# Loading a ring of weights in two transfers over 64 partitions each, instead of one over 128

## The chip, the cores and the metric

The kernel runs on one core of a Trainium2 chip. The metric is the device time of one execution, in microseconds. Before the change the median of three runs is 747.68 us (747.62 to 747.77).

## What is computed

The input is one image of 16 channels and 64 x 64 pixels in fp32. Four layers follow each other: a local normalisation with a blur of 13 x 13 (L0), a window attention block (L1), two 3 x 3 convolutions with a residual (L2), and the window attention block once more with other weights (L3). Almost all bytes of the problem are the weights of the two attention blocks. Cut to its matrix products, one block is:

```python
fl = _ln(xf, pn_g, pn_b)                          # 64 tokens of 1024
pw = _attn(fl, Wqk_p, PDH)                        # Wqk_p 1024 x 2048
pv = _heads(fl @ Wv_p)                            # Wv_p  1024 x 1024
pf = _merge(pw @ pv + _dwconv(pv, ...)) @ Wout_p  # Wout_p 1024 x 1024
ww = _attn(_ln(pl, pln_g, pln_b), Wqk_w, WDH)     # Wqk_w 1024 x 2048
wv = _heads(_ln(xw, wn_g, wn_b) @ Wv_w)           # 4 windows; Wv_w 16384 x 1024, 64 MB
wf = _merge(nds @ wv + _dwconv(wv, ...)) @ Wout_w # Wout_w 1024 x 16384, 64 MB
out = diag_scaled @ _heads(pf) + wf + x
```

## The kernel before

All weights are streamed from HBM once, in slots of 128 partitions x 2048 fp32 values (1 MB, 8 KB in each partition). One layer has 152 slots. `ring` in SBUF holds 16 of them, in two halves of 8 slots, b = 0 and b = 1; `extra` holds 4 more, for the first and the last slots ahead of the two big matrices. A load of a whole half is 128 rows of 64 KB, one for each partition, from one contiguous piece of 8.39 MB in HBM (`halves`). Some loads take half of a half (4 slots, 128 rows of 32 KB).

SP issues every DMA, all on one queue. Its program is written out by hand: `load_half` (line 268) waits for nothing itself; ahead of each call SP waits until PE has counted `slots_used` so far that the half is free. Each transfer counts up `half_landed[b]`, and a transfer that is whole adds 16. The other transfers of the program are: the first loads (`images`, `blurs`), five loads of `extra` from `ends`, the small inputs (`window_gains`, `small` over 104 partitions, `const`, `const_low` over 32, `l2w` over 16), six last pieces of the last matrix (`last`, over 128 partitions, line 305), two stores of `out` (28 partitions each) and two of `windows_last`. With the 37 ring loads that makes 59 transfers, 54 of them over 128 partitions.

PE works slot by slot. `half_there` (line 324) makes it wait on `half_landed[b]` before the first slot of a half. In the stage of Wv_w (line 490) each of 64 slots is multiplied by the staged window pixels and accumulated in one PSUM bank; in the stage of Wout_w (line 517) eight slots make a group, which ScalarE copies out (line 658), PE transposes (line 322) and VectorE adds to the image (line 937). After each slot PE counts up `slots_used`. The small first part of each layer (lines 386 to 474) works on the slots of the four small matrices, and between the two layers stands the convolution (lines 539 to 544).

Of the kernel before, what the change touches and what calls it, by code (L numbers as in the profile page):

```python
# [22 lines left out]
P = 128  # L23
# [10 lines left out]
SLOT = 2048  # L34
QUARTER = 4
HALF = 8
# [18 lines left out]
N_HALVES = (TURN + N_VW + N_OUTW) // HALF  # L55
# [5 lines left out]
def piece_at(n):  # L61

    at = sum(4 * (c1 - c0) * (h1 - h0) for c0, c1, h0, h1 in LAST_PIECES[:n])
    c0, c1, h0, h1 = LAST_PIECES[n]
    return at, at + 4 * (c1 - c0) * (h1 - h0)
# [52 lines left out]
def build(nc, images, blurs, const, const_low, window_gains, small, l2w, ends, halves, last, out, windows_last):  # L118
    with ExitStack() as ctx, ExitStack() as engines:
        def sb(name, *shape):  # L120
            return ctx.enter_context(nc.sbuf_tensor(name, list(shape), F32))

        def sem(name):
            return ctx.enter_context(nc.semaphore(name))


        ring = sb("ring", P, TURN * SLOT)
# [53 lines left out]
        half_landed = [sem(f"half_landed{b}") for b in range(2)]  # L181
# [50 lines left out]
        def used(L, s):  # L232

            return L * PER_LAYER + s
# [20 lines left out]
        @block.sync  # L255
        def _(sp):
            def load_end(L, n):
                lo = 0 if L or n else SLOT
                sp.dma_start(extra[:, lo:], ends[2 * L + n][:, lo:]).then_inc(extra_landed, 16)

            def load_small():
                sp.dma_start(area[0][:, :], window_gains).then_inc(gains_landed, 16)
                sp.dma_start(area[1][0:2 * N_SMALL, 0:P], small).then_inc(small_landed, 16)
                sp.dma_start(cst[:, C_WIDE:C_LOW], const).then_inc(const_landed, 16)
                sp.dma_start(cst[0:LOW, C_LOW:], const_low).then_inc(const_landed, 16)
                sp.dma_start(l2[:, :], l2w).then_inc(l2_landed, 16)

            def load_half(L, t, b, lo=0, hi=HALF):

                sp.dma_start(ring[:, (b * HALF + lo) * SLOT:(b * HALF + hi) * SLOT],  # L270
                             halves[t * 2 + (L * N_HALVES + 2 + b)][:, lo * SLOT:hi * SLOT]).then_inc(half_landed[b], 16)

            for L in range(2):
                load_end(L, 0)
                if L == 0:
                    load_small()
                if L:
                    sp.wait_ge(slots_used, used(L, -HALF))
                load_half(L, -1, 0)
                if L:  # L280
                    sp.wait_ge(slots_used, used(L, 0))
                else:
                    sp.wait_ge(image_turned, 1)
                load_half(L, -1, 1)
                sp.wait_ge(slots_used, used(L, QUARTER))
                load_end(L, 1)

                sp.wait_ge(slots_used, used(L, 2 * QUARTER))
                load_half(L, 0, 0, 0, QUARTER)
                sp.wait_ge(slots_used, used(L, 3 * QUARTER))  # L290
                load_half(L, 0, 0, QUARTER, HALF)
                sp.wait_ge(slots_used, used(L, 5 * QUARTER))
                load_half(L, 0, 1)
                with sp.Fori(1, 2 * TURNS - L) as t:
                    for b in range(2):
                        sp.wait_ge(slots_used, t * TURN + (used(L, S_VW) + b * HALF - HALF))
                        load_half(L, t, b)

            t = 2 * TURNS - 1
            sp.wait_ge(slots_used, used(1, S_VW) + t * TURN - HALF)  # L300
            load_half(1, t, 0)
            for n, landed in enumerate(last_landed):
                lo, hi = piece_at(n)
                sp.wait_ge(slots_used, used(1, S_VW) + t * TURN - HALF + (hi + SLOT - 1) // SLOT)
                sp.dma_start(ring[:, HALF * SLOT + lo:HALF * SLOT + hi], last[:, lo:hi]).then_inc(landed, 16)

            sp.wait_ge(rows_copied, 2)
            for wy in range(2):
                sp.dma_start(out[wy], out_rows[wy * WIN:wy * WIN + LAST, :]).then_inc(rows_stored, 16)
            sp.wait_ge(wide_copied, 1)  # L310
            sp.dma_start(windows_last[:, 0:WIDE], area[5][:, 0:WIDE]).then_inc(rows_stored, 16)
            sp.wait_ge(last_copied, 1)
            sp.dma_start(windows_last[:, WIDE:BANK], area[5][:, WIDE:BANK]).then_inc(last_stored, 16)
# [3 lines left out]
        def _(pe):  # L317
# [6 lines left out]
            def half_there(L, t, b):  # L324

                fills = (N_HALVES // 2 + 1, N_HALVES // 2)[b]
                before = 1 if t is None else (3, 2)[b]
                pe.wait_ge(half_landed[b], (0 if t is None else t) * 16 + 16 * (L * fills + before))

            def first_there(L, s):  # L330
                if s in (0, S_VW - QUARTER):
                    pe.wait_ge(extra_landed, 16 * (2 * L + (3 if s else 2)))
                elif s in (QUARTER, QUARTER + HALF):
                    half_there(L, None, s // HALF)
# [48 lines left out]
            with pe.Fori(0, 2) as L:  # L383
# [74 lines left out]
                for h in range(HEADS):  # L458
                    b, h2, hh, a = h % 2, h // 2, h // 4, h % 4 // 2
# [22 lines left out]
                with pe.Fori(0, TURNS) as i:  # L482
                    for k in range(TURN):
                        if k % HALF == 0:
                            pe.wait_ge(staged, i * 2 + (2 * TURNS * L + k // 8 + 1))
                            half_there(L, i, k // HALF)
                        w = slot_of(S_VW + k).rearrange("p (j n) -> p j n", j=4)
                        for j in range(4):
                            at = k % 8 * 8 + j // 2 * 4
                            m = mm(bank[0][32 * j:32 * j + 4, :], stage[:, k // 8, at:at + 4], w[:, j], start=False, stop=False)  # L490
                        m.then_inc(slots_used, 1)
# [17 lines left out]
                def group(L, i, g):  # L509
                    for h in range(GROUP):  # L510
                        if h == 0 and g == 0:
                            pe.wait_ge(wf_ready, L + 1)
                        if h == 0:
                            half_there(L, i + TURNS, g)
                        w = slot_of(S_OUTW + g * GROUP + h).rearrange("p (j n) -> p j n", j=4)
                        for j in range(4):
                            m = mm(bank[6 + g][32 * j:32 * j + 32, :], wf_t[:, h, :], w[:, j],  # L517
                                   start=(h == 0), stop=(h == GROUP - 1))
                        m.then_inc(slots_used, 1)
                    return m  # L520
# [494 lines left out]
```

## Time and profile before

| | |
|---|---|
| median of the runs | 747.68 us |
| the profiled execution, its own time | 747.75 us |
| its span in the profile | 746.4 us |
| mean granted TensorE clock | 0.783 |
| busy: PE, PE weight loads, VectorE, ScalarE, GpSimd | 58%, 17%, 12%, 5%, 1% of the span |
| DMA queue of the loads | 99.5% of 16 engines |
| moved | 320.51 MB, mean 429 GB/s |

The page of the profile divides the span in 40 slices of 18.7 us and gives each engine's busy share in tenths. A wait is put down to the work that ended it. The chain of work that ended last is followed back from the last instruction, at each step to what released it. Matmuls of fp32 data stand twice in the counts.

### The profile page before, as it was taken

The numbers are of one execution on the slowest core, as the hardware profiler recorded it, in microseconds if no ns is written. First come the engines' busy times: TensorE is split into PE (matmuls) and PEld (weight loads), VectorE is DVE, ScalarE is ACT, GpSimd is POOL, SyncE is SP. The second block draws the span as 40 slices with busy tenths as digits, with TensorE's granted clock in tenths as the row PEclk, the third lists the DMA queues.
The fourth block names the chain that finished last, engine by engine and source line by source line (L and its number), as shares of the span: only waits on it lengthen the run. The fifth ranks groups of instructions, "written<-read, shape, count | busy, mean of one in ns | idle before, by whom it ended". The sixth has DMA issues, their size and how long they took to land.

```text
span 746.4 us, 6899 instructions
## 1 busy us (share of the span) xinstructions
PE 430.1 (58%) x3011; PEld 129.0 (17%) x3011; DVE 90.9 (12%) x254; ACT 38.3 (5%) x80; POOL 9.3 (1%) x21
## 2 busy tenths in 40 slices
PE   6599854444446445455476988445444454544548
PEld 5233200000001111111122332000000011111113
DVE  2765300000002000000005171000000020000000
ACT  2111100000000000000001111000000000000000
POOL 2100000000000000000001000000000000000000
PEclk9579877777777776776789999877777777877879
DMA  9999999999999999999999999999999999999998
GB/s 396 436 403 429 459 411 439 443 439 421 435 446 412 435 440 443 425 428 446 418 432 443 417 431 446 446 421 425 446 435 421 439 446 421 425 446 435 421 423 350
DMA packets 8068, 320.51 MB, mean 429 GB/s; under 512 B 1065, under 2 KB 1601, under 8 KB 2169
## 3 DMA queue, kind: packets, MB, share of 16 engines
q1 hardware_dynamic: 8057, 320.35, 99.5%
q8 instruction: 8, 0.13, 0.1%
q14 instruction: 3, 0.02, 0.0%
HBM read 319.86 MB, written 0.49 MB: 429 GB/s over the span
## 4 chain that ended last, share of the span: by engine, by line
DMA 64%; PE 31%; DVE 3%; ACT 1%; issue 1%; SPq 0%; DVEq 0%; ACTq 0%
DMA ring<-halves 59%; PE bank L490 10%; PE bank L517 9%; PE bank L409 4%; DMA ring<-last 4%; PE bank L426 2%; PE bank L418 2%; DMA cst<-blurs 1%; PE bank L541 1%; PE bank L394 1%; PE bank L340 1%; PE bank L322 0%; DVE ring L724 0%; PE bank L386 0%; PE bank L539 0%
## 5 line engine op out<-in xcount | busy, mean ns | idle before, releaser
L490 PE MATMUL bank<-ring,stage 128*4 128x512 f32 x1024 | 140.8, 712 | 141.2 <-DMA ring<-halves 141.2
L517 PE MATMUL bank<-ring,wf_t 128*32 128x512 f32 x960 | 135.1, 726 | 128.4 <-DMA ring<-halves 128.4
L517 PEld LDWEIGHTS bank<-ring,wf_t 128*32 128x32 f32 x960 | 33.2, 131 | 219.9 <-DMA ring<-halves 121.8
L490 PEld LDWEIGHTS bank<-ring,stage 128*4 128x4 f32 x1024 | 26.9, 97 | 254.6 <-DMA ring<-halves 154.2
L937 DVE TENSOR_TENSOR image<-bank,image 128x32 f32 (+1 forms) x30 | 5.1, 193 | 275.9 <-PE bank L322 275.9
L902 DVE COPY wv_t<-bank 128x32 f32<-128x32 f32 x2 | 0.4, 190 | 286.6 <-PE bank L322 286.6
L322 PE MATMUL bank<-ident,area 128*128 128x128 f32 (+1 forms) x117 | 18.4, 284 | 12.2 <-ACT area L658 11.1
L658 ACT COPY area<-bank 128x512 f32<-128x512 f32 x15 | 8.8, 585 | 279.6 <-PE bank L517 279.6
L409 PE MATMUL bank<-extra,area 128*64 128x512 f32 x64 | 18.8, 752 | 3.8 <-DVE area L811 3.8
L474 PE MATMUL bank<-extra,area 128*64 128x512 f32 x64 | 18.4, 740 | 2.0 <-DVE area L876 2.0
L322 PEld LDWEIGHTS bank<-ident,area 128*128 128x128 f32 (+1 forms) x117 | 12.5, 141 | 31.7 <-ACT area L658 23.8
L646 ACT COPY stage<-area 128x64 f32 x16 | 3.9, 242 | 217.9 <-PE bank L490 203.8
L426 PE MATMUL bank<-ring,pooled_n 128*32 128x512 f32 x128 | 14.6, 595 | 0.0
L852 DVE SCALAR_TENSOR_TENSOR conv_p<-v_pad,vec,conv_p 128x636 f32<-128x636 f32 x16 | 14.1, 880 | 0.4
L418 PE MATMUL bank<-ring,area 128*64 128x512 f32 x64 | 14.1, 592 | 0.0
L409 PE MATMUL bank<-ring,area 128*64 128x512 f32 x64 | 14.1, 592 | 0.0
L561 PE MATMUL bank<-ring,wf_t 128*32 128x384 f32 (+1 forms) x128 | 7.9, 382 | 1.1 <-DMA ring<-last 1.1
L409 PEld LDWEIGHTS bank<-extra,area 128*64 128x64 f32 x64 | 5.6, 170 | 15.5 <-issue 15.5
L340 PE MATMUL bank<-cst,ring 128*128 128x128 f32 x16 | 3.8, 431 | 7.4 <-DMA cst<-blurs 7.4
L474 PEld LDWEIGHTS bank<-extra,area 128*64 128x64 f32 x64 | 5.5, 167 | 13.4 <-issue 13.4
L692 POOL TENSOR_TENSOR area<-area,vec 128x512 f32<-128x512 f32 x2 | 2.1, 1042 | 393.9 <-DVE area L786 393.9
L394 PE MATMUL bank<-area,ones 128*128 128x512 f32 x4 | 3.9, 1090 | 4.3 <-ACT area L612 4.3
(202 smaller groups left out, 206.8 us busy)
## 6 DMA issues: line engine op xcount, KB each, us to landing
ring<-halves SPq DMA_DIRECT2D x4, 4096.0 KB, 20.1
extra<-ends SPq DMA_DIRECT2D x3, 4096.0 KB, 16.4
extra<-ends SPq DMA_DIRECT2D x1, 3072.0 KB, 12.4
ring<-last SPq DMA_DIRECT2D x1, 3072.0 KB, 22.5
ring<-last SPq DMA_DIRECT2D x2, 1536.0 KB, 25.9
extra<-ends SPq DMA_DIRECT2D x1, 1024.0 KB, 4.9
ring<-last SPq DMA_DIRECT2D x1, 1024.0 KB, 28.9
ring<-last SPq DMA_DIRECT2D x1, 768.0 KB, 29.9
```

The lines of the kernel that those rows point to most:

```text
L322: return mm(dst, src, ident[0:rows, 0:rows], start=True, stop=True, is_transpose=True)
L340: m = mm(bank[pair // 4][:, pair % 4 * P:pair % 4 * P + P], l0_in[:, 2 * pair:2 * pair + 2, :].rearrange("p c x -> p (c x)"), cc("blur_y") ...
L394: mm(bank[0][:, :], ones, area[1][:, :], start=True, stop=True).then_inc(var_sums, 1)
L409: m = mm(bank[4 + m2][b * 64:b * 64 + 64, :], fl[:, s - S_QKP, :], w[:, m2, b], start=(s == S_QKP), stop=(s == S_VP - 1))
L418: m = mm(bank[6][b * 64:b * 64 + 64, :], fl[:, kt, :], w[:, t, b], start=(kt == 0), stop=(kt == KT - 1))
L426: m = mm(bank[7][32 * j:32 * j + 32, :], pooled_n[:, s - S_QKW, :], w[:, j * BANK:(j + 1) * BANK], start=(s == S_QKW), stop=(s == S_OUTP - 1))
L474: m = mm(bank[4][f * 64:f * 64 + 64, :], a3(8, TOK)[:, h, :], w[:, t, f], start=(h == 0), stop=(h == HEADS - 1))
L490: m = mm(bank[0][32 * j:32 * j + 4, :], stage[:, k // 8, at:at + 4], w[:, j], start=False, stop=False)
L517: m = mm(bank[6 + g][32 * j:32 * j + 32, :], wf_t[:, h, :], w[:, j], start=(h == 0), stop=(h == GROUP - 1))
L561: m = mm(dst, wf_t[:, h, :], w[:, h - h0, j], start=(h == 0 and c0 == 0), stop=(h == HEADS - 1))
L658: sc.copy(area[4 + g][:, :], bank[6 + g][:, :]).then_inc(group_copied, 1)
L852: then(v.scalar_tensor_tensor(conv_p[:, 0:159, 0:4], src, wt, conv_p[:, 0:159, 0:4], ALU.mult, ALU.add))
```

## The change

Each load of the ring is issued as two DMAs, one over partitions 0 to 63 and one over partitions 64 to 127, with the same columns, one right behind the other on SP's queue. Both count up the same semaphore, so PE now waits for 32 for each load instead of 16. Nothing else is changed; the loads of `extra`, the last pieces, the small inputs and the stores stay whole.

```diff
             def load_half(L, t, b, lo=0, hi=HALF):
 
-                sp.dma_start(ring[:, (b * HALF + lo) * SLOT:(b * HALF + hi) * SLOT],
-                             halves[t * 2 + (L * N_HALVES + 2 + b)][:, lo * SLOT:hi * SLOT]).then_inc(half_landed[b], 16)
+                for rows in (slice(0, P // 2), slice(P // 2, P)):
+                    sp.dma_start(ring[rows, (b * HALF + lo) * SLOT:(b * HALF + hi) * SLOT],
+                                 halves[t * 2 + (L * N_HALVES + 2 + b)][rows, lo * SLOT:hi * SLOT]).then_inc(half_landed[b], 16)
...
                 before = 1 if t is None else (3, 2)[b]
-                pe.wait_ge(half_landed[b], (0 if t is None else t) * 16 + 16 * (L * fills + before))
+                pe.wait_ge(half_landed[b], (0 if t is None else t) * 32 + 32 * (L * fills + before))
```

Before the change, the body of SP's loop over the ring (two halves; ISA and REGISTER_ALU are register instructions) and the load behind it read:

```order
L270 ISA [waits slots_used]
L270 DMA ring<-halves 128x16384
L296 REGISTER_ALU
L270 ISA [waits slots_used]
L270 DMA ring<-halves 128x16384
L294 REGISTER_ALU
L294 COMPARE_AND_BRANCH
L259 DMA extra<-ends 128x8192
```

With the change the same place on SP reads (every line number is one higher):

```order
L271 ISA [waits slots_used]
L271 DMA ring<-halves 64x16384
L271 ISA
L271 DMA ring<-halves 64x16384
L297 REGISTER_ALU
L271 ISA [waits slots_used]
L271 DMA ring<-halves 64x16384
L271 ISA
L271 DMA ring<-halves 64x16384
L295 REGISTER_ALU
L295 COMPARE_AND_BRANCH
L259 DMA extra<-ends 128x8192
```

Each wait on `slots_used` is followed by two transfers, with a register instruction between them. On the other engines no instruction moves.

## Rows read from the trace of the kernel before

**Rows 1.** The page: PE's busy time, and the DMA's share and rate by slice.

```profile
PE 430.1 (58%) x3011; PEld 129.0 (17%) x3011; DVE 90.9 (12%) x254; ACT 38.3 (5%) x80; POOL 9.3 (1%) x21
...
DMA  9999999999999999999999999999999999999998
GB/s 396 436 403 429 459 411 439 443 439 421 435 446 412 435 440 443 425 428 446 418 432 443 417 431 446 446 421 425 446 435 421 439 446 421 425 446 435 421 423 350
```

**Rows 2.** The page: DMA packets, and the queue of the loads.

```profile
DMA packets 8068, 320.51 MB, mean 429 GB/s; under 512 B 1065, under 2 KB 1601, under 8 KB 2169
...
q1 hardware_dynamic: 8057, 320.35, 99.5%
```

**Rows 3.** The page: shares of the chain that ended last.

```profile
DMA 64%; PE 31%; DVE 3%; ACT 1%; issue 1%; SPq 0%; DVEq 0%; ACTq 0%
DMA ring<-halves 59%; PE bank L490 10%; PE bank L517 9%; PE bank L409 4%; DMA ring<-last 4%; PE bank L426 2%; PE bank L418 2%; DMA cst<-blurs 1%; PE bank L541 1%; PE bank L394 1%; PE bank L340 1%; PE bank L322 0%; DVE ring L724 0%; PE bank L386 0%; PE bank L539 0%
```

**Rows 4.** The same chain by time: start us, us, what.

```profile
104.82 9.79 PE bank L490 x64
...
114.78 28.71 DMA ring<-halves
...
191.04 29.86 DMA ring<-halves
```

**Rows 5.** Timeline of PE: start us, us, then in brackets the idle time before.

```profile
104.82 9.74 PE L490 MATMUL bank<-ring,stage 128*4 128x512 f32 x64 [8.97 <-DMA ring<-halves]
124.18 8.60 PE L490 MATMUL bank<-ring,stage 128*4 128x512 f32 x64 [9.62 <-DMA ring<-halves]
143.53 9.16 PE L490 MATMUL bank<-ring,stage 128*4 128x512 f32 x64 [10.75 <-DMA ring<-halves]
162.89 9.72 PE L490 MATMUL bank<-ring,stage 128*4 128x512 f32 x64 [10.20 <-DMA ring<-halves]
```

**Rows 6.** Stretches of one turn each, three of seven; last PEclk, DMA share, GB/s.

```profile
104.82:143.53 38.71, 18.34 (x128) 3.41 (x129) 0.00 (x0) 0.49 (x2) 0.00 (x0) 0.72 1.00 433
...
298.35:337.04 38.69, 19.03 (x136) 5.14 (x136) 0.69 (x4) 1.17 (x2) 0.00 (x0) 0.76 1.00 434
...
666.27:704.98 38.71, 19.75 (x137) 5.31 (x137) 0.69 (x4) 1.17 (x2) 0.00 (x0) 0.76 1.00 433
```

**Rows 7.** DMA issues: operation, count, KB each, median us from issue to landing.

```profile
ring<-halves SPq DMA_DIRECT2D x4, 4096.0 KB, 20.1
...
ring<-halves SPq DMA_DIRECT2D x33, 29.5
...
out<-extra SPq DMA_DIRECT2D x2, 112.0 KB
...
cst<-const SPq DMA_DIRECT2D x1, 61.0 KB, 11.8
area<-small SPq DMA_DIRECT2D x1, 52.0 KB
cst<-const_low SPq DMA_DIRECT2D x1, 36.0 KB, 11.9
l<-l2w SPq DMA_DIRECT2D x1, 18.1 KB, 11.6
```

**Rows 8.** Line 270: durations in ns, min/median/max.

```profile
L270 SPq DMA_DIRECT2D ring<-halves x37: 327/333/422, 5.3 to 695.2; - x37
L270 SPq FUSED_REGOPS  x26: 52/54/67, 95.9 to 675.3; - x26
```

**Rows 9.** Waits of SP: who, on what, us in total, times, longest.

```profile
SPq L270 <- PE bank L490: 302.3, 16, 22.6
SPq L270 <- PE bank L517: 242.9, 13, 19.6
```

**Rows 10.** Timeline of PE in the tail.

```profile
724.44 8.86 PE L517 MATMUL bank<-ring,wf_t 128*32 128x512 f32 x64 [9.66 <-DMA ring<-halves]
...
743.37 1.08 PE L561 MATMUL bank<-ring,wf_t 128*32 128x128 f32 x32 [0.77 <-DMA ring<-last]
```

## The prediction

> **What bounds the kernel now.** I read the page first. The DMA row of the forty slices is 9 in every slice but the last, and the bytes row stays between 396 and 459 GB/s until then [rows 1]. The one queue that carries the loads, q1, takes 99.5% of the time of sixteen engines [rows 2]. No compute engine comes near that: PE is busy for 58% of the span [rows 1]. The chain that ended last gives 64% to DMA, 59% to the loads that this change touches, and 31% to PE [rows 3]. That 31% could mislead, so the second view is the chain in order of time. It alternates: PE works for some 9 us on one half of the ring, SP issues the refill of that half the moment it is free, and the chain then follows that refill for some 29 us to its landing [rows 4]. But the refill is not moving bytes for 29 us: it stands behind the refill of the other half. PE's own timeline shows the pace: groups start at 104.82, 124.18, 143.53 and 162.89 us, so a half lands every 19.35 us, PE needs 8.6 to 9.7 us for it, and PE is idle before each group on the DMA [rows 5]. The third view measures whole turns of the ring, two halves each: 38.70 or 38.71 us, with the DMA share at 1.00 and 433 or 434 GB/s, in both layers and in both kinds of stage [rows 6]. That is two times 8.39 MB in 38.71 us, 433.4 GB/s, or 27.1 GB/s for each of sixteen engines. The kernel is one uninterrupted stream of loads at a fixed rate, and its time is bytes divided by that rate. Only the first microseconds and the tail are anything else.
>
> **What the change adds.** Bytes, order and destinations are the same. There are 37 transfers at this line, 33 of a whole half and 4 of half of one [rows 7], worth 33 + 4 / 2 = 35 whole halves; each is now two.
>
> First, SP. It issues 37 DMAs more, and one register instruction more with each of the 26 that the loops issue. An issue takes 0.33 us (median), a register instruction 0.05 us [rows 8]. The second transfer is issued some 0.4 us after the first, while the queue holds most of another half: the refill reaches its landing 28.7 to 29.9 us after its issue though its own share of the stream is 19.35 us, so some 10 us of older work lie ahead of it [rows 4]. SP itself waited 302.3 and 242.9 us on PE at this line [rows 9]. So the cost is nothing. If that cover were gone it would be 37 x 0.38 = 14 us.
>
> Second, the completions. The 1065 packets below 512 B [rows 2] are the 128 rows of the constants (61.0 KB in 128 rows is 488 B each) and 937 completion writes. The program has 59 transfers: 54 over 128 partitions, and five over 104, 32, 16, 28 and 28 [rows 7]. With 16 completions for each of the 54, 864, there are 73 left for the five, and 13 + 16 + 16 + 14 + 14 = 73: each is spread over the largest number up to 16 that divides its partitions. So a transfer over 64 partitions is spread over 16 engines too, 4 rows each, instead of 8 rows each. That matters: the two transfers don't go to two sets of eight engines side by side; all sixteen take the lower one and then the upper one. The 37 x 16 = 592 added completion writes carry 4 bytes each. For their cost the nearest row is the whole queue: 8057 packets at 99.5%, in which 937 such writes leave a rate of 433 GB/s. I take nothing, at most 0.5 us.
>
> Third, and this decides, the destination. Before, at each moment the sixteen engines together write into all 128 partitions. After, they write into 64, then into the other 64. No row of this profile shows a large transfer into half of the partitions, so this has to be bounded from both sides. The lower end is nothing: if 27.1 GB/s is what an engine can move whatever its target, the stream stays at 433 GB/s. The upper end is a halving: if 27.1 GB/s is a sixteenth of what the 128 partitions can take in, and 64 partitions can take in half of that, two engines share each entry and the stream falls to 217 GB/s while all engines are in the same half. Then each half of the ring costs 19.35 us more, and the sum is 35 x 19.35 = 677 us. The nearest rows, the turns of the ring [rows 6], fit both ends, since every transfer in them uses all partitions. What they say is that the limit is a hard one: 38.69 to 38.71 us in seven turns, whatever PE, VectorE and ScalarE were doing. Such a constant belongs to a path of fixed width, and the destination is one of two places where it can lie. I take the halving.
>
> The Trainium skill speaks against the change here. "SBUF — State Buffer", section "Door 1: The DMA port swizzle", says that partitions 0 to 63 reach only the eight even ones of sixteen write ports, and 64 to 127 the eight odd ones, each about 27 GB/s; it gives 196 GB/s at 1 MiB for partitions 0 to 63, and 218 GB/s as the limit for large transfers. Its section "Can I just issue two DMAs to hit both halves?" says no: two concurrent ones gained 6% over one. From the 218 GB/s one would estimate 293.6 MB of ring loads at 1347 us, where 436 GB/s gives 673 us. No run here shows any of it yet.
>
> **Where the stall goes.** PE waits longer before each group: a half lands every 38.7 us and takes PE 9 to 10. PE's clock: in these turns the granted clock is 0.72 to 0.76 [rows 6], a mix of the levels of 1.2 and 2.4 GHz, and idleness precedes each group. With longer idleness more of a group may run at the lower level; were all of it there, a group of 9.7 us would take under 20 us, still inside 38.7 us, so it costs nothing in the loop. At the end, under the last pieces, which are not split, PE is idle for 9.66 us before its last group and again before the last piece at 743.37 us [rows 10]; a slower clock could cost a microsecond or two there. The loads of the extra slots and the last pieces stay as they are.
>
> **The sum.** The profiled execution took 747.75 us for a span of 746.4 us; the median of the runs is 747.68 us, so the two agree to 0.1 us. 747.7 + 677 + 0 (SP) + 0 (completions) = 1425 us.
>
> **The rivals.**
> The engines drift apart. The halving holds only while the two engines that share an entry are in the same half of the partitions. If one gets ahead, each has its entry to itself for that stretch. With a share f of the time so spent, a half takes 19.35 x (2 - f): f = 0.25 gives 1256 us, f = 0.5 gives 1086 us, f = 0.75 gives 917 us. The 10 us of queued work leave room for it [rows 4]. Against it: fair sharing keeps a lead as it is and doesn't build one up, and a half counts only when the slowest pair has finished.
> The destination is no limit. Then nothing changes but hidden issues, and the time is 747.7 us, at most 748.5. For it speaks that the mean rate of each engine is the same in every view; against it, that nothing in the rows puts the limit into the engines.
> It gets faster. The one way is a higher rate of the stream, since its idle time is next to nothing: if the sixteen engines read and write a range half as wide more easily than the whole one, and the rate rose by 1% from 433 GB/s, 677 us would shrink by 6.8 us, to 741 us. It decides from a gain of 0.2% in the rate on, 1.5 us. The turns at 433 or 434 GB/s without exception speak for a ceiling [rows 6], and nothing in the change raises one.
>
> **How the numbers follow.** The halving with the engines nearly in step gets 0.63, its own range 1380 to 1440 us. The drift gets 0.20, spread over 765 to 1380 us. No change gets 0.13, faster 0.04. The forecast is 1425 us. The range from 850 to 1440 us holds the halving and most of the drift, 0.63 + 0.17 = 0.80, and leaves out the rest. About 0.2% (1.5 us) is what a measurement of this kernel can tell from no change. Slower by more than that: 0.63 + 0.20 = 0.83. Within it: 0.13. Faster: 0.04.
>
> **What would show it.** In the profile after, a turn of the ring should take 77.4 us at about 217 GB/s with the DMA share still at 1.00, since the engines are held up in their writes and not idle. PE's 31 groups should start 38.7 us apart, PE's busy share should fall to near 30%, and issue to landing should roughly double from 29.5 us [rows 7]. Completion packets should rise by 592, the first stage's DMA into other tiles should look as before. A turn between 40 and 75 us says drift, 38.7 us says that the destination is no limit. The forecast is wrong if the limit of 27.1 GB/s is the engine's own; then every later number but SP's falls with it.

## The result, and the profile after

The changed kernel takes 1484.45 us (median of 4 runs, 1479.78 to 1485.67) against 747.69 us before, a ratio of 1.984 (95% interval 1.982 to 1.987): 736.8 us slower. The forecast of 1425 us was right in kind and too low in size, and the time lies above the top of its range, 1440 us. The profiled execution has a span of 1482.1 us.

From the page of the changed kernel, the busy shares, the granted clock, the DMA's busy share, its rate by slice, the packets and the queue, which answer to [rows 1, 2]:

```profile
PE 446.5 (30%) x3011; PEld 131.4 (9%) x3011; DVE 91.1 (6%) x254; ACT 38.2 (3%) x80; POOL 9.3 (1%) x21
...
PEclk8766566655565566566677675566555566656667
DMA  9999999999999999999999999999999999999998
GB/s 285 199 257 222 202 216 207 200 218 205 200 218 206 200 216 207 202 216 205 214 258 205 238 225 217 214 210 200 216 207 210 212 202 216 207 210 212 200 216 283
DMA packets 8661, 320.52 MB, mean 216 GB/s; under 512 B 1657, under 2 KB 2193, under 8 KB 2761
...
q1 hardware_dynamic: 8649, 320.35, 99.8%
```

The DMA is as busy as before, in every slice, and moves the same bytes at half the rate. This is the line to learn from: a busy share of 99.8% does not say that the engines work at their rate, since an engine that is held up counts as busy too. The trace's records of single packets say the same. A row of 64 KB is one packet, 4224 of them in each kernel: it took 2.42 us on average before (2.42 to 3.08) and 5.03 us now, and only one of the 4224 took less than 4 us. The small packets went from 1065 to 1657, by 592 = 37 x 16, so each added transfer does post sixteen completions and is spread over sixteen engines. From issue to landing a load of 64 rows takes 63.1 us (median), where a whole one took 29.5 us.

Three whole turns of the ring in the stage of Wv_w (stretch, us, busy times, granted clock, DMA share, GB/s), for [rows 6]:

```profile
190.81:271.54 80.73, 17.06 (x128) 3.26 (x128) 0.00 (x0) 0.49 (x2) 0.00 (x0) 0.63 1.00 208
271.54:352.28 80.74, 18.23 (x128) 3.42 (x128) 0.00 (x0) 0.49 (x2) 0.00 (x0) 0.61 1.00 208
352.28:433.05 80.77, 19.43 (x129) 3.56 (x130) 0.00 (x0) 0.24 (x1) 0.00 (x0) 0.58 1.00 208
```

A turn takes 80.74 us where it took 38.71 us and where I had forecast 77.4 us. Per half of the ring that is 40.37 us instead of 19.35 us; 35 x 21.02 = 736 us, which is the whole difference of 736.8 us. So the loss sits in the ring loads alone. The tail has no part in it: from the start of PE's last group of 64 matmuls to the end of the span it is 21.8 us, and it was 22.0 us.

PE's timeline, for [rows 5], shows where the stall went:

```profile
190.81 8.38 PE L491 MATMUL bank<-ring,stage 128*4 128x512 f32 x64 [30.59 <-DMA ring<-halves]
231.18 8.68 PE L491 MATMUL bank<-ring,stage 128*4 128x512 f32 x64 [31.99 <-DMA ring<-halves]
271.54 8.97 PE L491 MATMUL bank<-ring,stage 128*4 128x512 f32 x64 [31.69 <-DMA ring<-halves]
```

A group is as long as before, 8.4 to 9.9 us, though the mean granted clock of a turn fell from 0.72 to between 0.58 and 0.63: the mean takes in the longer idle time. What grew in these turns is the idle time before a group, from about 10 to about 31 us. Over the whole kernel PE is busy for 446.5 us instead of 430.1 us, in good part in the first part of a layer, where it now waits before groups that it ran without a pause before (line 427: 770 ns for a matmul, 595 ns before); the stream hides that too. SP's issues became dearer, which I had not expected, and stayed hidden, as its waits on PE show (line 271, ns min/median/max; then the waits):

```profile
L271 SPq DMA_DIRECT2D ring<-halves x74: 465/474/604, 5.2 to 1390.6; - x74
...
SPq L271 <- PE bank L491: 639.2, 16, 49.2
```

In the chain that ended last the loads now stand as "another core or an unknown queue", 65%. There is no other core in this program; it is the same stretches between two groups of PE that [rows 3] give to `ring<-halves`, and PE's own wait still names `ring<-halves`, which is the one to read.

### The profile page after: what moved, and what is told of

Its sections match the earlier page's. It is cut to its first block, busy times and chain, and to the rows that moved or that the text cites. A ratio compares the mean times of both kernels' runs of the same rounds, so it can differ in the third digit from the quotient of the medians.

```text
span 1482.1 us, 6988 instructions
## 1 busy us (share of the span) xinstructions
PE 446.5 (30%) x3011; PEld 131.4 (9%) x3011; DVE 91.1 (6%) x254; ACT 38.2 (3%) x80; POOL 9.3 (1%) x21
## 2 busy tenths in 40 slices
DMA packets 8661, 320.52 MB, mean 216 GB/s; under 512 B 1657, under 2 KB 2193, under 8 KB 2761
## 3 DMA queue, kind: packets, MB, share of 16 engines
q1 hardware_dynamic: 8649, 320.35, 99.8%
## 4 chain that ended last, share of the span: by engine, by line
another core or an unknown queue 65%; PE 27%; DMA 4%; DVE 3%; ACT 1%; issue 0%; SPq 0%; ACTq 0%; DVEq 0%
PE bank L491 10%; PE bank L518 9%; DMA ring<-last 3%; PE bank L410 2%; PE bank L475 1%; PE bank L419 1%; PE bank L323 1%; PE bank L427 1%; DVE conv_p L853 1%; ACT area L659 1%; DMA cst<-blurs 0%; PE bank L542 0%; PE bank L341 0%; PE bank L395 0%
## 5 line engine op out<-in xcount | busy, mean ns | idle before, releaser
L491 PE MATMUL bank<-ring,stage 128*4 128x512 f32 x1024 | 145.8, 733 | 486.6 <-DMA ring<-halves 486.6
L427 PE MATMUL bank<-ring,pooled_n 128*32 128x512 f32 x128 | 19.7, 770 | 44.6 <-DMA ring<-halves 44.6
L410 PE MATMUL bank<-ring,area 128*64 128x512 f32 x64 | 18.9, 758 | 17.6 <-DMA ring<-halves 17.6
L475 PE MATMUL bank<-extra,area 128*64 128x512 f32 x64 | 17.5, 708 | 2.0 <-DVE area L877 2.0
L419 PE MATMUL bank<-ring,area 128*64 128x512 f32 x64 | 14.1, 592 | 0.0
L427 PEld LDWEIGHTS bank<-ring,pooled_n 128*32 128x32 f32 x128 | 4.4, 130 | 55.3 <-DMA ring<-halves 45.1
L410 PEld LDWEIGHTS bank<-ring,area 128*64 128x64 f32 x64 | 5.5, 174 | 31.0 <-DMA ring<-halves 19.3
## 6 DMA issues: line engine op xcount, KB each, us to landing
ring<-halves SPq DMA_DIRECT2D x66, 63.1
```

The costliest lines, as they stand in the source:

```text
L410: m = mm(bank[4 + m2][b * 64:b * 64 + 64, :], fl[:, s - S_QKP, :], w[:, m2, b], start=(s == S_QKP), stop=(s == S_VP - 1))
L419: m = mm(bank[6][b * 64:b * 64 + 64, :], fl[:, kt, :], w[:, t, b], start=(kt == 0), stop=(kt == KT - 1))
L427: m = mm(bank[7][32 * j:32 * j + 32, :], pooled_n[:, s - S_QKW, :], w[:, j * BANK:(j + 1) * BANK], start=(s == S_QKW), stop=(s == S_OUTP - 1))
L475: m = mm(bank[4][f * 64:f * 64 + 64, :], a3(8, TOK)[:, h, :], w[:, t, f], start=(h == 0), stop=(h == HEADS - 1))
```

## The experiments

All but two_queues change only the lines of the change. Where the number of transfers differs, PE's wait is for 16 times that number. In all of them row r of the piece in HBM goes to partition r, as in the two kernels compared. Each diff shows only the lines that make the difference.

### Two transfers, split by columns

```diff
+                mid = (lo + hi) // 2
+                for a, z in ((lo, mid), (mid, hi)):
+                    sp.dma_start(ring[:, (b * HALF + a) * SLOT:(b * HALF + z) * SLOT],
+                                 halves[t * 2 + (L * N_HALVES + 2 + b)][:, a * SLOT:z * SLOT]).then_inc(half_landed[b], 16)
```

> Each ring load goes as two transfers again, but split by columns: 128 partitions x 4 slots and 128 partitions x 4 slots, so the number of transfers, completions and issues is that of the changed kernel. Main theory (half of the partitions take in only half of the stream): 747.7 us within 0.2%, a turn of the ring 38.7 us, 433 GB/s. Rival (the price is one of the number of transfers or completions): up to 1484 us.

Measured: 750.58 us, ratio 1.0038 (1.0023 to 1.0052). A turn takes 38.86 us, at 432 GB/s. As many transfers, issues and completions as in the changed kernel, over all partitions, cost next to nothing; the rival falls. The 2.9 us are more than my 0.2%: a turn is 0.15 us longer, 17.5 turns give 2.6 us. What differs is that each row is 32 KB instead of 64 KB, so that there are twice as many packets of data; evenodd below, with as many transfers and rows of 64 KB, costs nothing.

### Three transfers: the middle 64 partitions, then the outer ones

```diff
+                for rows in (slice(32, 96), slice(0, 32), slice(96, P)):
```

> Each ring load as three transfers: partitions 32 to 95, then 0 to 31, then 96 to 127. Main theory in the form of the Trainium skill (SBUF - State Buffer, Door 1: partitions 0 to 63 have one set of eight write ports and 64 to 127 the other): 32 to 95 reach all sixteen, at full rate 9.7 us, the two pieces of 32 rows reach eight each, 9.7 to 10.1 us each; 29.0 to 29.9 us for a half, 747.7 + 35 x 9.7 to 10.5 = 1087 to 1116 us. Rival 1 (the rate goes with the number of partitions, wherever they are): 64 rows at half the rate 19.4 us, each 32 rows at a quarter 19.4 us, 58 us for a half, 2100 us. Rival 2 (the cause is on the side of HBM, where a transfer now reads a contiguous piece of 4.2 MB instead of 8.4 MB): the middle piece is as slow as in the changed kernel, and the total 1484 us or more.

Measured: 1355 us (1350 and 1360). None of the three numbers. The groups of PE start 37.0, 39.5, 40.8 and 43.3 us apart where I had expected 29 to 30 us, and unlike in the other kernels that move all the bytes the engines have idle time. The windows of two turns, and the queue over the whole kernel:

```profile
201.49:281.86 80.37, 18.23 (x129) 3.43 (x129) 0.00 (x0) 0.49 (x2) 0.00 (x0) 0.61 1.02 241
281.86:363.44 81.58, 17.91 (x129) 3.35 (x129) 0.00 (x0) 0.49 (x2) 0.00 (x0) 0.60 0.82 216
...
q1 hardware_dynamic: 9241, 320.36, 88.4%
```

The DMA share is 0.82 in the second turn and 88.4% over the kernel. This run alone does not tell the theories apart; the next ones do.

### Four transfers of 32 neighbouring partitions

```diff
+                for rows in (slice(0, 32), slice(32, 64), slice(64, 96), slice(96, P)):
```

> Each ring load as four transfers of 32 partitions in order. Main theory (0 to 31 reach as many ports as 0 to 63): each quarter at the same 208 to 217 GB/s, 1425 to 1490 us in all, like the changed kernel. Rival (the rate goes with the number of partitions): a quarter of the rate, 747.7 + 35 x 58 = 2780 us.

Measured: 1487.6 us (1485.1 and 1490.0), a turn 80.77 us at 208 GB/s. The number of partitions in a transfer does not set the rate: 32 are as fast as 64.

### Two transfers: the even and the odd partitions

```diff
+                for rows in (slice(0, P, 2), slice(1, P, 2)):
```

> Each ring load as two transfers over 64 partitions each, the even ones (0, 2, ... 126) and the odd ones. Main theory: the even partitions reach all ports, so the full rate is possible, 747.7 us, unless the engines walk over their four rows in step and meet at the same ports (then anything up to 1484 us). Rival (64 partitions are slow wherever they are): 1484 us. With the first result the sets of ports are shown to matter and not the count.

Measured: 747.78 us, ratio 1.0000 (0.9990 to 1.0011). PE's timeline:

```profile
162.93 9.65 PE L491 MATMUL bank<-ring,stage 128*4 128x512 f32 x64 [10.26 <-DMA ring<-halves]
182.29 8.51 PE L491 MATMUL bank<-ring,stage 128*4 128x512 f32 x64 [9.71 <-DMA ring<-halves]
```

and the turn that they begin:

```profile
162.93:201.64 38.71, 18.16 (x128) 3.41 (x128) 0.00 (x0) 0.49 (x2) 0.00 (x0) 0.72 1.00 433
```

19.36 us for a half, the pace of before. This is the decisive pair with the changed kernel: the same 74 transfers of 64 rows of 64 KB (and of 32 KB), the same completions and the same bytes. Only which partitions, and with them which rows of HBM, stand together differs, and 737 us hang on it.

### Four transfers of every fourth partition

```diff
+                for rows in (slice(a, P, 4) for a in range(4)):
```

> Each ring load as four transfers of 32 partitions each, every fourth partition from 0, 1, 2 and 3 on. Main theory (they reach all sixteen ports, and evenodd ran at the full rate): 747.7 us, within 0.3%. Rival (32 partitions are slow, or four transfers instead of one cost something): above 755 us, up to the 1487 us of quarters.

Measured: 747.89 us, ratio 1.0001 (0.9991 to 1.0012). 148 transfers of 32 partitions instead of 37 of 128 cost nothing that can be measured. Beside quarters, 1487.6 us, it is the same contrast once more.

### Only the lower, only the middle, only the outer partitions

These leave out half of the bytes of all ring loads but the first two. only_low and only_mid have one transfer for each load; only_outer has two, partitions 0 to 31 and 96 to 127.

```diff
+                rows = slice(0, P) if L == 0 and isinstance(t, int) and t < 0 else slice(0, 64)    # or slice(32, 96)
```

> Leaves out half of the bytes: all ring loads but the first two cover only partitions 0 to 63 (the other partitions keep old weights). One transfer for each load, as before the change. Main theory: each half takes 19.4 to 20.2 us for half of the bytes, so the time is about that of the kernel before, 740 to 780 us, at 208 to 217 GB/s. Rival (the slowness comes from having two transfers that get in each other's way): 9.7 us for a half, then bound by PE and the chain, about 400 to 480 us.

> The same, but the one transfer covers partitions 32 to 95. Main theory: the full rate, 9.7 us for a half of the ring, about as long as PE needs for it (8.6 to 9.8 us), 400 to 480 us in all. Rival (64 partitions are slow wherever they are): the same as only_low, 740 to 780 us.

> Leaves out half of the bytes: all ring loads but the first two cover only partitions 0 to 31 and 96 to 127, as two transfers. Main theory: each of them 10.1 us, 20.2 us for a half of the ring, 786 us like only_low. Then middle should have cost 9.7 + 20.2 = 29.9 us for a half, and what it took beyond that comes from the mixing of the two kinds of transfer. Rival (two pieces of 32 rows are slower than one of 64): the excess of middle is here, 27 us for a half, about 1020 us.

Measured: 786.5, 508.8 and 810.1 us. The first two lie 6.5 and 29 us above their ranges, the third 24 us above its forecast. Windows of whole turns, of the lower and of the outer partitions:

```profile
150.19:191.00 40.81, 17.24 (x129) 3.25 (x130) 0.00 (x0) 0.49 (x2) 0.00 (x0) 0.75 1.00 206
```

```profile
170.69:210.66 39.97, 17.73 (x129) 3.34 (x129) 0.00 (x0) 0.49 (x2) 0.00 (x0) 0.76 1.00 210
```

The lower 64 partitions take 20.40 us for half of the bytes of a half of the ring: a single transfer, with nothing to get in its way, runs at 206 GB/s. For the middle 64 partitions, PE's timeline reads:

```profile
106.58 9.28 PE L491 MATMUL bank<-ring,stage 128*4 128x512 f32 x64 [5.80 <-DMA ring<-halves]
116.24 7.05 PE L491 MATMUL bank<-ring,stage 128*4 128x512 f32 x64 [0.39 <-DMA ring<-halves]
128.66 8.48 PE L491 MATMUL bank<-ring,stage 128*4 128x512 f32 x64 [5.37 <-DMA ring<-halves]
```

22.1 us for two halves, about half of the 40.8 us of the lower partitions, with hardly any wait before every second group; windows there show 373 to 383 GB/s with a DMA share of 0.9. The packets tell it without PE's share in it: one of 64 KB takes 2.42 us (median), as in the kernel before, and 5.1 us in only_low. PE is busy for 79% of the span of only_mid, and no load is always waiting in the queue (85.8% of sixteen engines), which fits the 29 us but was not tested. So 64 partitions are not slow as such: 32 to 95 are fast, and so are the even ones.

The outer ones behave in the turns as expected, 20.0 us. The 24 us over only_low lie in the start: for the first two loads this kernel uses two transfers of 64 partitions, and only_low one of 128. PE's first group of the Wv_w stage, in only_low and in only_outer:

```profile
89.06 7.05 PE L491 MATMUL bank<-ring,stage 128*4 128x512 f32 x64 [1.15 <-DMA ring<-halves]
...
130.72 9.96 PE L492 MATMUL bank<-ring,stage 128*4 128x512 f32 x64 [5.61 <-DMA ring<-halves]
```

It starts 41.7 us later, which is two loads at 21 us more each. Each later half is some 0.4 us shorter (20.0 instead of 20.4 us), 13 us in all, which leaves 28 us, near the 24 us measured. So two transfers of 32 rows are no slower than one of 64, and by its parts the middle kernel should have taken 9.7 + 20.0 = 29.7 us for a half. The 7 us beyond it ((1355 - 747.7) / 35 + 19.35 = 36.7 us) come from mixing the kinds.

### Eight transfers of 16 neighbouring partitions

```diff
+                for rows in (slice(a, a + 16) for a in range(0, P, 16)):
```

> Each ring load as eight transfers of 16 neighbouring partitions. Main theory (16 neighbouring partitions reach four of sixteen ports; a port takes 27.1 GB/s, shared by four engines): 108.4 GB/s, 77.4 us for a half, 747.7 + 35 x 58.05 = 2780 us. If the loss by sharing of only_low and quarters (some 205 GB/s instead of 217 GB/s) holds here too: about 2930 us. Rival (the loss is one of 32 and 64 partitions only, or the limit is a whole side of 64 partitions): 1490 us.

Measured: 2542.8 us (2528.5 and 2557.1). A turn:

```profile
320.57:466.10 145.53, 17.36 (x129) 3.30 (x129) 0.00 (x0) 0.49 (x2) 0.00 (x0) 0.57 1.00 115
```

115 GB/s, a little over a quarter of 433; the time is 237 us under the 2780 us of the main theory. The step from 32 to 16 neighbours costs what the step from 64 to 32 did not. The rival falls. It is faster than the 108.4 GB/s of four entries. Neighbouring transfers may overlap, since here the engines can get ahead of each other across more borders, but that is only argued.

### Changing sides more often, and a second queue

Lower and upper partitions alternate for every 4 slots (halves_of_32k) or for every slot (fine); in two_queues twelve loads are split between SP and ScalarE, and its programs for SP, ScalarE and PE are changed for that.

```diff
+                for a in range(lo, hi, 4):    # or 1
+                    for rows in (slice(0, P // 2), slice(P // 2, P)):
```

> Like the changed kernel, but each half of the ring is loaded in two steps of four slots, lower then upper side in each, with rows of 32 KB; the engines change side every 10 us instead of every 20. Theory A (time is won back at each change of side, where some engines are ahead of others): fine won 19.35 + 2 x 7.2 to 3.9 us by eight times as many changes, so twice as many should win a little, 1420 to 1475 us. Theory B (fine was faster because of its short rows): 1480 to 1500 us, since rows of 32 KB are still long.

> Each ring load in slots: 0 to 63 then 64 to 127 for each slot, 16 transfers with rows of 8 KB for a whole half. The engines then change side every 1.2 to 2.6 us, less than the several microseconds by which their descriptors are offset from each other. Theory A (the engines that share a port keep their offset, and are then in different halves part of the time): well under 1484 us, 900 to 1300 us. Theory B (the engines are brought into step at each change of side, or the limit is on the whole side): 1425 to 1500 us, plus what small rows cost.

> Only the loads of turns 1 to 3 of the Wv_w stage in each layer are split (12 of the 35 whole halves), the lower 64 partitions issued by SP and the upper 64 by ScalarE on its own queue, at the same moment; all others are whole as before. If both split transfers ran on one queue, those 12 would cost 12 x 21 = 252 us more, 1000 us. Theory A (an engine with work on two queues alternates between them, so at each moment some write the lower and some the upper side): between 748 and 900 us. Theory B (all engines alternate in step): 1000 us.

Measured: halves_of_32k 1464.9 us (1464.2 and 1465.7). That is 19.5 us less than the changed kernel, 0.6 us for a half, and inside the range of theory A. fine had two runs far apart, 1236 and 1347 us; its profile is of the slower, with this turn:

```profile
177.00:249.98 72.98, 18.47 (x129) 3.45 (x129) 0.00 (x0) 0.49 (x2) 0.00 (x0) 0.62 1.02 230
```

two_queues had 976 and 1002 us; in its profile, of the slower, the split stretch runs like this, with all engines busy:

```profile
162.17:240.81 78.64, 17.60 (x128) 3.37 (x129) 0.00 (x0) 0.49 (x2) 0.00 (x0) 0.61 1.00 214
```

So a second queue gives back 2 of the 42 us that a turn loses, and in the faster run, by its time, about twice that ((975.7 - 747.7) / 12 = 19.0 us for a split half, where the changed kernel loses 21.0 us). Both runs lie within 24 us of the 1000 us of theory B and outside the range of theory A. That the engines keep in step is how theory B explains it; no view shows the engines one by one. With short pieces part of the loss is won back, 137 us to 248 us in fine, as theory A has it. Short rows as such don't do that, since those of columns cost 0.4%. In fine's profile SP's 560 issues stand for 29% of the chain that ended last, though the DMA is busy throughout, so more than the change of sides may be at work there. That it is the offset between engines which does it was not measured by itself, and why fine's two runs differ by 9% stays open.

## Why the prediction was wrong in its size, point by point

**What bounds the kernel: right.** The stream of loads is everything: time before and after is 35 halves times the pace of the stream, plus a constant.

**SP and completions: right.** evenodd has the same 74 transfers at a ratio of 1.0000, every_fourth 148 at 1.0001. One issue is not 0.33 us but 0.474 us in the changed kernel, and none of it shows.

**Sixteen engines for each transfer: right,** by the 592 small packets.

**The destination halves the stream: right in kind.** That it depends on which partitions are loaded together is shown; that the limit is at the destination is argued. The rival "the destination is no limit", which leaves the engines' own rate as the only limit, is refuted by only_low (206 GB/s), and "it gets faster" by the result. But the mechanism as I put it, "64 partitions can take in half" of what 128 can, was too coarse. It is neither the number of partitions (every_fourth, 32 at the full rate) nor of transfers (columns) nor the piece of HBM that one transfer reads (quarters reads neighbouring rows of 2.1 MB, the changed kernel 4.2 MB, at one rate, and only_mid reads 4.2 MB fast). It is which partitions stand together: 0 to 63 are as slow as 0 to 31, 32 to 95 have packets as fast as all (2.42 us), 16 neighbours are little more than half as fast as 32.

One rival no run tests. Row r in HBM always goes to partition r, so a limit that goes with the addresses read, and not with the partitions written, would show the same pattern if it had the same groups; a load that puts neighbouring rows of HBM into scattered partitions would tell the two apart. That the limit is on the side of the destination is therefore argued. What speaks for it is a map of the destination that was there before these runs.

The map in "SBUF — State Buffer", section "Door 1: The DMA port swizzle", of the Trainium skill gives this order, eight ports for 0 to 31 and for 0 to 63, sixteen for 32 to 95, four for 16 neighbours, and the rates of these runs stand in this order: 208, 206, full and 115 GB/s. Of the section "Can I just issue two DMAs to hit both halves?" of the same page one sentence does not hold here: "The only way to hit all 16 ports is one transfer spanning all 128 partitions." Two transfers of 64 partitions each, the even and the odd ones, ran at 433 GB/s, the rate of one transfer over all 128.

**The failed step is the size of the halving.** The prediction has "the stream falls to 217 GB/s", and from it 19.35 us for each half, 677 us in the sum. It falls to 208 GB/s, and the term is 35 x 21.02 = 736 us. I had divided the rate by two and assumed, without a row for it, that two engines that share an entry lose nothing by it. The halved stream is slower than half: only_low 206 GB/s, quarters 208, only_outer 210, where 216.7 would be half of the 433.4. The loss of 3 to 5% does not come from changing sides, since it is there in only_low, where the engines never do. Nor does it lie in gaps: the DMA share of these turns is 1.00, and a packet of 64 KB takes 5.03 us on average in the changed kernel where twice 2.42 us would be 4.84 us. Its inner cause was not looked into. The second fault was the range: I closed the top at 1440 us, 1% over the forecast, although I had named the sharing as the unknown; that one engine can move 27.1 GB/s into an entry of its own says nothing about two in turns.

**The engines drift apart: not in the changed kernel.** An engine with an entry to itself should move its row in some 2.4 us, as in the kernel before, and only one packet of 4224 took less than 4 us; nor do the turns, 80.73 to 80.77 us, get shorter. The borders between kinds are where something moves: for the better in halves_of_32k and fine, for the worse in middle.

**Open:** where the 7 us of middle go. The queue is busy for 88.4%, so of the 36.7 us of a half some 4.3 us are idle time, and the rest, about 2.7 us, is in packets that take longer than in the kernels with one kind of transfer. That some engines run out of work while others are still held up, so that a half is complete only when the last engine is, would fit; no run isolates it.

## What to carry to other kernels

A large transfer into SBUF that is split by partitions should keep partitions from all over the array in each part (every second, every fourth: free, 747.8 and 747.9 us); a split into neighbouring blocks below and above partition 64 halves the rate of a stream that is at its limit, and blocks of 16 cut it to about a quarter. Read GB/s beside the DMA's busy share: 99.5% and 99.8% were 429 and 216 GB/s. And where a forecast divides a rate between sharers, leave room on both sides: in place of a clean half the rate was 3 to 5% lower, in place of a clean quarter 6% higher (115 instead of 108.4 GB/s).

## What the runs showed that I had not expected

The halved stream runs some 4% below half (208 GB/s instead of 216.7). An issue takes SP 474 ns in the changed kernel where it took 333 ns [rows 8]; it is 475 ns in evenodd and in only_low but 316 ns in quarters, 473 ns in every_fourth and 333 ns in columns, so it does not follow the number of partitions alone, and I can't say what it follows. Rows of 32 KB instead of 64 KB cost 0.4% of the stream (38.86 us for a turn instead of 38.71). Two executions of fine on one chip differ by 9%, while those of the kernel before agree within 0.1%.
